# A recurrent attention step on TensorE: one product of zeros per step taken out

## What is computed

```
def step(carry, ht):                                   # 256 times, one after the other
    H_prev, H_prev_tilde = carry                       # the last 5 inputs and outputs
    temp = jnp.tanh(H_prev @ W1 + (ht @ W2)[:, None, :] + H_prev_tilde @ W3)
    w_t = jax.nn.softmax(temp @ v, axis=1)
    ht_hat = jnp.sum(H_prev_tilde * w_t, axis=1)
    ht_tilde = ht + jax.nn.relu(ht_hat)
    ...                                                # both windows move on by one
# then, for every token: y = sum over e of comb[e] * (gelu(x @ W1[e] + b1[e]) @ W2[e] + b2[e])
```

## Time and profile before

| | |
|---|---|
| median of three runs | 580.36 us (577.89 to 582.26) |
| the profiled execution | 582.32 us, of which 580.4 us are its span |
| TensorE, products | busy 557.9 us, 96% of the span, 6331 instructions |
| VectorE | busy 413.3 us, 71% |
| ScalarE | busy 354.0 us, 61% |
| granted TensorE clock, mean | 0.941 of full |
| the 255 single products of zeros | one per step of the recurrence, from 90 to 558 us |

### The profile page before, as it was taken

How to read it: one execution, slowest core, us unless ns; L and a number is a source line. 1 busy time by engine, 2 the same in 40 slices (tenths; PEclk the granted TensorE clock), 3 DMA queues, 4 the chain that set the end, 5 groups by cost and what they waited for, 6 DMA issues and landing times. The chain is left out here.

```text
span 580.4 us, 19441 instructions
## 1 busy us (share of the span) xinstructions
PE 557.9 (96%) x6331; PEld 446.0 (77%) x6331; DVE 413.3 (71%) x2867; ACT 354.0 (61%) x1440; POOL 47.4 (8%) x101
## 2 busy tenths in 40 slices
PE   6999879999999999999999999999999999999987
PEld 3555436778888888888888888888888888888875
DVE  2456555777777878787877787878787877777763
ACT  2335645556666666666666666666666666666654
POOL 1000000010101010101010101010101010101010
PEclk9555569999999999999999999999999999999999
DMA  8000000000000000000000000000000000000000
GB/s 228 17 2 1 0 0 3 2 3 2 3 6 3 6 3 7 3 7 3 6 3 6 3 6 3 7 3 7 2 6 3 6 3 7 2 7 3 8 2 10
DMA packets 7507, 5.84 MB, mean 10 GB/s; under 512 B 1216, under 2 KB 6896, under 8 KB 7408
## 3 DMA queue, kind: packets, MB, share of 16 engines
q1 hardware_dynamic: 6784, 4.57, 2.8%
q10 hardware_dynamic: 528, 0.03, 0.1%
q0 software_dynamic: 96, 0.00, 0.0%
HBM read 3.55 MB, written 1.05 MB: 8 GB/s over the span
## 5 line engine op out<-in xcount | busy, mean ns | idle before, releaser
L470 ACT ACTIVATE th<-bank 128x32 f32<-128x32 f32 x255 | 51.3, 201 | 145.4 <-PE bank L696 145.4
L938 DVE TENSOR_TENSOR_SCAN CC<-th,DE 128x16 f32<-128x16 f32 x510 | 115.3, 226 | 0.5 <-issue 0.5
L728 PE MATMUL bank<-f,hid 128*128 128x128 f32 x512 | 112.9, 302 | 1.0 <-ACT hid L492 0.6
L497 ACT ACTIVATE GF<-Z,cst 64x32 f32<-64x32 f32 x255 | 105.4, 413 | 11.7 <-DVE Z L989 2.5
L942 DVE SCALAR_TENSOR_TENSOR DE<-CC,yh 128x40 f32<-128x40 f32 x509 | 81.9, 203 | 27.2 <-DVE yh L1005 0.5
L938 DVE TENSOR_TENSOR_SCAN C<-th,DE 128x16 f16<-128x16 f32 x255 | 49.3, 193 | 73.0 <-ACT th L470 68.3
L633 PE MATMUL bank<-xnT,f1p 128*128 128x128 f16 x1024 | 99.2, 219 | 0.2 <-ACT hid L492 0.2
L696 PE MATMUL bank<-Tf,v 128*128 128x32 f32 x510 | 99.3, 277 | 0.0
L685 PE MATMUL bank<-Tf,nv 128*128 128x32 f32 x510 | 98.9, 276 | 0.0
L492 ACT ACTIVATE hid<-bank,b1T 128x128 f32<-128x128 f32 x256 | 94.4, 369 | 5.7 <-PE bank L633 4.8
L694 PE MATMUL bank<-GF,cst 128*128 128x32 f32 x510 | 95.3, 269 | 0.0
(11 more groups left out here) (135 smaller groups left out, 827.3 us busy)
## 6 DMA issues: line engine op xcount, KB each, us to landing
x_tok<-in_x_dram SPq DMA_DIRECT2D x4, 256.0 KB, 4.3
f<-in_L_ffn_W_dram SPq DMA_DIRECT2D x1, 1024.0 KB
out_dram<-acc SPq DMA_DIRECT2D x16, 64.0 KB
w<-in_L_attn_W_dram SPq DMA_DIRECT2D x3, 64.0 KB, 3.9
cst<-shape_constants_dram SPq DMA_DIRECT2D x1, 148.5 KB, 2.5
wfg<-in_L_conv_Wf_dram ACTq DMA_DIRECT2D x1, 8.0 KB, 2.3
wfg<-in_L_conv_Wg_dram ACTq DMA_DIRECT2D x1, 8.0 KB, 2.3
bhc<-in_L_conv_bh_dram POOLq DMA_DIRECT2D x1, 0.1 KB, 3.4
```

Of the source, the lines that this page charges most:

```text
L470: act.activation(th[p][:, 0:W4, 1], psS[p][:, 0:W4], ACT.Tanh, bias=-K0 / 2, scale=0.5 / WS).then_inc(th_ready, 1)
L497: act.activation(GF[p][0:NODES, :], Z[p][0:NODES, :], ACT.Tanh, bias=half_nodes, scale=half_nodes).then_inc(f_ready, 1)
L728: mm = pe.matmul(psO[e % 2][:, 0:D], hid[u % 2][:, :], f2[:, u, :], start=(half == 0), stop=(half == HH - 1))
L938: return dve.tensor_tensor_scan(flat[0], flat[1], flat[2], 0.0, ALU.mult, ALU.add)
```

## The change

One line is taken out of the step:

```diff
                         product(in5(psA[p][:, 0:W5]), w3w, relu, False, True, ALL_PRODUCTS[2:]).then_inc(projected, 1)
                         h_products(k, i, q)
-                        keep_busy(psS[p], 256, 1)
 
                         pe.wait_ge(g_ready, n)
                         pe.wait_ge(f_ready, n)
```

## The result

The changed kernel takes 779.35 us, the median of four runs (775.13 to 784.24), against 581.31 us of the kernel before (577.89 to 583.29, four runs): a ratio of 1.342, interval 1.331 to 1.352. The forecast of 580 was wrong, and rival one of the prediction, the clock, is what came.

The account below looks back on a forecast made before the run. The prediction took a chain round TensorE, ScalarE and VectorE as the bound; 582.32 us profiled plus 0 for regular steps, late steps and restart gave 582.3, in the median 580.4, rounded to 580; range 575.5 to 587.5 us.

Parts of the forecast that it names:

- rival one: TensorE in the recurrence: more pause drops its clock to half, giving 723 to 850 us; chance one in ten.
- What bounds the kernel, and what the fold waits for: Recurrence: a chain round three engines sets 1.84 us a step; the fold waits for the nodes' tanh, not the zeros.
- The late step's count: Fold behind L671: it starts 0.10 us behind the zeros' start, against 0.20 in regular steps, so 0.10 is other waiting.
- The direct gain of 0: Recurrence steps: removing the zeros gains 0 in some 238 regular steps and 0, at most 0.3 us, in late ones.
- rival three: Fold after a pause of the array: costs 0.03 us more a step, 7.7 us in all, so 588 us; chance 0.04.
- The sum: Whole kernel: 0 for regular steps, late steps and restart, so 582.3 us profiled and 580.4 us in the median.
- The price of the fall: TensorE's step at half clock: 1.44 us of work becomes up to 2.9, +1.06 us a step.
- The lower bound of +0.56: Recurrence step at half clock: +0.56 us if only TensorE's work on the chain doubled.

Follow-up runs that it names:

- e5_end: Kernel before, its 256 columns of zeros moved from ahead of the fold to TensorE's step end: 578.84, 632.08, 738.42 and 787.57 us.
- e9_wide: Kernel before with two products of 256 columns of zeros ahead of the fold instead of one: ratio 1.0005, ten runs.
- e16_both: Kernel before, its zeros replaced by six 8-column products ahead of the fold and 256 columns at step end: 647.05, 816.55, 582.39 and 861.70 us.
- e11_192: Kernel before with 192 columns of zeros ahead of the fold instead of 256: 590.59, 580.89, 574.97 and 576.97 us.
- e8_cold: Kernel before without the 33 products of 512 columns that raise the clock ahead of the recurrence: 596.57 us, one run.
- e1_moved: Kernel before, its 256 columns of zeros moved from ahead of the fold to behind L695: 652.98, 628.94, 784.23 and 784.34 us.

## Why the prediction was wrong, point by point

- **What bounds the kernel, and what the fold waits for: right.** The 0.12 us from the nodes' tanh to the fold stood with no product of zeros (0.11 at 102 us after the change, 0.12 in `e5_end`) and with two (`e9_wide`). The late step's count, 0.10 for the zeros and 0.10 of spare time, held too: a second product of some 0.11 us cost nothing.
- **The direct gain of 0: right.** Steps at the upper level take 1.82 us with and without zeros. The dearer fold (rival three) did not show: from the load of L695 to th are 0.45 us at 102 us too.
- **The sum: wrong, since it left the clock at the upper level.** The failing step is the clock, which the sum put at nothing on the weight of rival one, "I give the fall one chance in ten". What the runs showed in its place: the clock fell in all four runs, at 127.3 us in the one with a trace, and some 230 steps cost 0.87 us more each, 199 us. The ground for the one in ten was the earlier trace rows: from 575 to 578 us TensorE was busy for 2.06 of 3.00 us and the clock stayed up. That was a short stretch behind a dense one (2.90 of 3.00 us from 572 to 575), and I let it speak for a load that lasts 468 us. It shows that the clock does not fall at once, not that a lighter step is safe. The other row of the same group, a stretch busy for 3.30 of 3.30 us with a fall at its end, was the one to follow: it had already said that busy time is no measure of what keeps the clock. No row of before showed, though, where between the two this step would lie.
- **The price of the fall: right in kind, a little too high at its upper end.** The prediction had TensorE's 1.44 us a step doubling to 2.9, +1.06 a step; measured are 2.61 and +0.79. The terms of long work doubled nearly as said, the fold 0.21 to 0.43 and L695 0.23 to 0.43. Others grew less: hp from 0.15 to 0.20, R from 0.06 to 0.08, the experts' four from 0.22 to 0.40. So the sum of 1.44 became 2.61 and not 2.9, and some 230 steps were slow rather than 255. The lower bound of +0.56, for the chain alone, was too low since TensorE became the bound. The result lies inside the rival's 723 to 850.
- **The Trainium skill's rule** on brief idling between groups of products ("TensorE: Matmul & The Clock Gate", section "A second HAM failure mode: psum-queue depth-cycling") pointed the right way, and the trace after agrees that the clock can be lost without a long pause: in the recurrence ahead of the fall TensorE's longest pause is 0.30 us. The section tells of swings between the levels; here the recurrence fell once and stayed down for 628 us, up to 755 us. And `e16_both` fell with no pauses to speak of, so brief pauses alone are not the measure either.
- **I said what would hide the product (the nodes' tanh) and took hidden for useless.** A product that costs nothing can still do something, and what it did here was not on the chain.

## What to carry to other kernels

Before taking out work that looks idle, ask what it does besides taking time: on TensorE the granted clock depends on it, and the stake here was not the instruction's microseconds but 34% on the kernel's time. Where filler is wanted, put it where the engine waits for another one on every turn of the chain: 512 columns were free ahead of the fold and cost 3% behind the score's product. Judge a margin over several executions: `e5_end`, `e11_192` and `e16_both` each had runs that kept the clock and runs that lost it, and one execution of each would have shown either by luck. And look for the longest step of the loop, not only the mean one.

## What the runs showed of the hardware

- A level of the clock can last by itself: in the changed kernel TensorE was busy for 622.70 of 622.70 us at 1.2 GHz and the clock did not rise, in `e8_cold` TensorE was busy for 49.00 of 49.00 us at 1.2 GHz and it did rise, at 141 us.
- Busy time in the profile does not show what keeps the clock: it fell behind a stretch with 171.36 of 171.50 us busy, and stayed up in `e5_end` where 244.64 of 250 were:

```profile
300.00:550.00 250.00, 244.64 (x3183) 212.27 (x3183) 193.50 (x1443) 164.79 (x712) 20.12 (x42) 1.00 0.02 5
```

- At half the clock a float32 product of 32 columns with its load of weights took 0.43 us for its two passes instead of 0.21 to 0.23; three float16 products of 40 columns 0.10 instead of 0.08.
- Runs of one and the same kernel differ: four runs of `e5_end` took 578.84 to 787.57 us, with mean granted clocks from 0.964 down to 0.611.
- Work that is free at the upper level is paid for at the lower: the 256 columns of zeros add nothing to a step of 1.82 us at 2.4 GHz, and 0.22 us at 1.2 GHz (2.83 in `e1_moved`, 2.61 in the changed kernel).
